# Storing the first shared results from ScalarE's queue, and a third pair of staging buffers

## Chip, cores and metric

The kernel runs on one core of a Trainium2 chip. Its time is the device time in microseconds (us) of one execution; several executions are timed and the median is given. The engines are called PE (TensorE, matmuls), DVE (VectorE), ACT (ScalarE), POOL (GpSimd) and SP (SyncE, which here only issues DMAs); SPq and ACTq are the instruction queues of SP and ACT.

## What is computed

The reference is one block of a network over an input of 4 batches of 1024 tokens with 256 features, all float32. It has two halves.

```
x = x + layernorm(mixer(layernorm(x)))           # linear, conv, scan over tokens, gated linear
x = x + layernorm(ffn(layernorm(x)))
def ffn(x):                                      # 4096 tokens of 256 features
    xn = layernorm(x) * gamma + beta
    top 2 of 8 experts per token, weights comb
    out = sum over e of comb[:, e] * swiglu(xn, gate_up[e], down[e])     # experts, 1024 hidden
    out = out + swiglu(xn, shared_gate_up, shared_down)                  # shared expert, 256 hidden
```

`swiglu` is `(silu(clip(gate)) * up) @ down`. The change touches the last line: the results of the shared expert and the way in which they reach the sum.

## The kernel before

**Two stages.** The first stage, the mixer (0 to about 478 us of the profile), works through the batches b = 0 to 3; each is two half batches of 512 tokens, numbered k = 2b + half, 0 to 7. Mixer, routing, splitting of the expert weights into a high and a low part, and the shared expert are interwoven here. The second stage (from 478 us) runs the routed experts in slots of 256 or 128 rows and adds their rows into `acc_dram` (named `acc_scratch` in the profile) by indirect DMAs from POOL. The shared expert's results must be in `acc_dram` before these additions begin: they are stored there, not added.

**The order is written out by hand.** `ORDER` is a table with one string for each engine; each word, such as `e0/1`, names a stage, its step and a batch or half batch, and `run` calls them in that order. An engine's queue is served in order, so a word that waits holds back all words behind it. For the change these words matter:

- `g`, `y` on PE: gate and up product (`sh_gate`) and down product (`sh_down`) of the shared expert, for half batch k and half f = 0, 1. `clip`, `times` on DVE and `s` on ACT lie between them.
- `ef/k` on ACT, so `e0/1` for half 0 of half batch 1: `sh_copy`, which copies the down product of 256 tokens from PSUM bank 4 to a staging buffer (128 x 512 float32) and counts `s_out` up. PE's next `y` waits for `s_out`, because it overwrites bank 4.
- `sh/k` on SP: `store_shared`, which for both f waits for `s_out` and stores the buffer (256 KB) to `acc_dram`, counting up `s_stored[buffer][f]` when it has landed.
- `n`, `st`, `xr`, `x` on SP: load the next raw piece of expert weights and store the two split parts of an earlier one; store the mixer's result `x1`; load the residual; load the next batch. `w` on ACT and DVE splits a piece.
- `be`, `exp`, `ln`, `abar`, `hi` on ACT, `dt`, `da`, `ac`, `bx`, `h` on DVE, and `dl`, `A`, `b` on PE: the eight units of the scan over tokens of each batch.

**The staging buffers are borrowed.** `sh` holds two pairs. Pair 0 is `a_cum` and `bx`, which the scan of the next batch writes too; pair 1 is the first half of `x_in`, free once the last batch has been normalised and turned. Half batches 0, 1 and 2 are done inside batches 1, 2 and 3 and use pair 0. So the first scan step of batch b (`acum_unit` and `bx_unit` with n = 0) waits on DVE until the store of half batch b - 1 has landed. Half batches 3 to 7 come at the end and alternate: 3, 5 and 7 use pair 1, 4 and 6 use pair 0. `sh_copy` waits for the last store out of its buffer to land, by `used(k)`.

**Signals before the first use.** The weights `w2`, `w3` and the router each have a semaphore in `w_full_loaded`; PE waits for each at its first use.

Of the kernel before, what the change touches and what calls it, by code (L numbers as in the profile page):

```python
# [12 lines left out]
P = 128  # L13
B, L, D, H = 4, 1024, 256, 512
# [3 lines left out]
HALF = 512  # L18
# [47 lines left out]
def mixer(nc, x, w_e, w_s, weights, full, consts, shared, xs_dram, x1_dram, acc_dram, fill, vec, ident,  # L66
# [3 lines left out]
    with ExitStack() as ctx:  # L70
# [80 lines left out]
        vec_loaded = sem("vec_loaded")  # L151
        w_full_loaded = [sem(f"w_full_loaded{i}") for i in range(len(full))]
        w_hi_ready, w_lo_ready = sem("w_hi_ready"), sem("w_lo_ready")
# [9 lines left out]
        s_clipped, s_silu, s_hid, s_out = sem("sh_clipped"), sem("sh_silu"), sem("sh_hid"), sem("sh_out")  # L163
        s_stored = [[sem(f"sh_stored{i}{f}") for f in range(2)] for i in range(2)]
        stats_seen = sp_seen = pool_seen = sem("mixer_waits_seen")
# [28 lines left out]
        def free(engine, what):  # L194
            if what == "x_ps":
                engine.wait_ge(yn_ready, 2 * B + 1)
            elif what == "gu_ps":
                engine.wait_ge(s_hid, 4 * B)
            elif what == "down_ps":
                engine.wait_ge(s_out, 4 * B)  # L200
                engine.wait_ge(slots_ready, B + 2)
            elif what == "xg":
                engine.wait_ge(s_done, 4 * B + 2)
                engine.wait_ge(cv_ready, 4 * B + 2)
            elif what == "gate":
                engine.wait_ge(xs_lo_ready, 4 * B)
                engine.wait_ge(plan_ready, 1)
            elif what == "tables":
                engine.wait_ge(plan_ready, 2)
            elif what == "x1":  # L210
                engine.wait_ge(x1_stored, 16 + 32 * B)
            elif what == "acc":
                engine.wait_ge(ends_cleared, 16 * (E + 2))
                for i in range(2):
                    for f in range(2):
                        engine.wait_ge(s_stored[i][f], 16 * sum(buf_of(k) == i for k in range(2 * B)))
# [33 lines left out]
        sh = [[a_cum[:, :].rearrange("p (t d) -> p t d", d=D), bx[:, :].rearrange("p (t d) -> p t d", d=D)],  # L250
              [x_in[:, 0:2, :], x_in[:, 2:4, :]]]

# [5 lines left out]
        def round_of(b, half):  # L258

            return (b, 0, LT) if b < B - 1 else (b + half, half * HT, HT)  # L260

        def hid_of(k):
            return hid[0 if k < B - 1 else k % 2]

        def buf_of(k):
            return 0 if k < B - 1 else k % 2

        def sh_of(k):
            return sh[buf_of(k)]

        def used(k):
# [89 lines left out]
        def _(sp):  # L361
# [24 lines left out]
            def store_shared(k):  # L386
                for f in range(2):
                    rows = slice(k * HALF + f * 2 * P, k * HALF + (f + 1) * 2 * P)
                    sp.wait_ge(s_out, 2 * k + f + 1)
                    sp.dma_start(acc_dram[rows, :].rearrange("(t p) d -> p t d", p=P), sh_of(k)[f]).then_inc(s_stored[buf_of(k)][f], 16)  # L390

# [29 lines left out]
            for n in range(1, len(full)):  # L421
                load_weights(w_full, *full[n], w_full_loaded[n])
            for at, src, chunks in shared:
# [44 lines left out]
        def _(pe):  # L468
# [69 lines left out]
            def d_stage(b, half, d):  # L538
# [20 lines left out]
                if d in (2, 3):  # L559
                    o = d - 2  # L560
                    if o == 0:
                        pe.wait_ge(s_ready, 2 * k + 2)
                        if k == 0:
                            pe.wait_ge(w_full_loaded[1], 16)
                    for c in range(DC):
                        i = full(banks[6 + o][:, :], W(w_full, W2_AT, c, D, o * P), s[:, c, :], c == 0, c == DC - 1)
                    i.then_inc(g_done, 1)
                if d in (4, 5):
                    if d == 4:
                        pe.wait_ge(z_ready, k + 1)  # L570
                        if k == 0:
                            pe.wait_ge(w_full_loaded[2], 16)
                    for t in ((0, 1), (2, 3))[d - 4]:
# [21 lines left out]
                if d == 9:  # L595
                    r, first, n = round_of(b, half)
                    pe.wait_ge(xnt_ready, 2 * k + 2)
                    if r == 0:
                        pe.wait_ge(w_full_loaded[3], 16)
                    for t in range(n):  # L600
# [44 lines left out]
        def _(act):  # L645
# [146 lines left out]
            def sh_copy(k, f):  # L792
                act.wait_ge(sd_done, 2 * k + f + 1)
                if used(k):
                    act.wait_ge(s_stored[buf_of(k)][f], used(k))
                nc.scalar.activation(sh_of(k)[f], banks[4][:, :].rearrange("p (t d) -> p t d", d=D), ACT.Copy).then_inc(s_out, 1)

            run("scalar", {"p": split_high, "N": normalise_x, "t": copy_xt, "u": copy_u, "c": conv_middle, "S": silu_cv, "r": round_xs,
# [5 lines left out]
        def _(dve):  # L804
# [221 lines left out]
            def sh_clip(k, f):  # L1026
                dve.wait_ge(sg_done, 2 * k + f + 1)
                if buf_of(k) == 0:
                    dve.wait_ge(h_lo_ready, min(k + 1, B) * NU + 2)
# [752 lines left out]
```

## Time and profile before

| | us |
|---|---|
| median of 3 timed executions | 1136.74 (1132.38 to 1138.24) |
| the profiled execution | 1142.15 |
| span in its profile, first to last instruction | 1140.4 |

The rows quoted further down come from the profiled execution alone. A row of the timeline has the start, the busy time, engine and line, the operation with its output and input, and in brackets the idle time of the engine ahead of it with what ended it.
### The profile page before, as it was taken

The numbers are of one execution on the slowest core, as the hardware profiler recorded it, in microseconds if no ns is written. First come the engines' busy times: TensorE is split into PE (matmuls) and PEld (weight loads), VectorE is DVE, ScalarE is ACT, GpSimd is POOL, SyncE is SP. The second block draws the span as 40 slices with busy tenths as digits, with TensorE's granted clock in tenths as the row PEclk, the third lists the DMA queues.
The fourth block names the chain that finished last, engine by engine and source line by source line (L and its number), as shares of the span: only waits on it lengthen the run. The fifth ranks groups of instructions, "written<-read, shape, count | busy, mean of one in ns | idle before, by whom it ended". The sixth has DMA issues, their size and how long they took to land.

```text
span 1140.4 us, 22452 instructions
## 1 busy us (share of the span) xinstructions
PE 1041.2 (91%) x7042; PEld 917.3 (80%) x7042; DVE 800.2 (70%) x2056; ACT 623.9 (55%) x1269; POOL 286.5 (25%) x302
## 2 busy tenths in 40 slices
PE   3889999989988999799999999999999999999940
PEld 2666677668567666599999999999999999999940
DVE  4987898897968766576666666666666666666645
ACT  6867868776767346254444444454444444444415
POOL 1133123552353163311112121211211211112125
PEclk9899999999988999999999999999999999999975
DMA  8655666875574578957363721736275911368139
GB/s 292 215 203 203 224 210 221 266 264 186 180 250 157 189 258 287 335 174 252 81 251 63 245 37 28 254 76 204 41 235 161 345 32 25 68 207 259 34 94 220
DMA packets 123563, 208.96 MB, mean 183 GB/s; under 512 B 9840, under 2 KB 75120, under 8 KB 123504
## 3 DMA queue, kind: packets, MB, share of 16 engines
q1 hardware_dynamic: 108096, 188.33, 48.1%
q0 software_dynamic: 15408, 19.93, 10.0%
q8 instruction: 27, 0.44, 0.2%
q14 instruction: 32, 0.26, 0.1%
HBM read 357.61 MB, written 85.50 MB: 389 GB/s over the span
## 4 chain that ended last, share of the span: by engine, by line
PE 72%; DVE 8%; issue 5%; SPq 5%; DMA 4%; POOL 3%; ACT 2%; ACTq 0%; DVEq 0%; POOLq 0%
PE bank L479 12%; PE bank L1443 8%; PE bank L1444 8%; PE bank L1445 8%; PE bank L1488 4%; PE bank L1490 4%; PE bank L1489 4%; PE bank L473 4%; PE bank L474 4%; PE bank L475 4%; POOL xs_scratch L1209 2%; DMA w_both<-w_split 2%; SPq L1310 2%; PE bank L1461 1%; PE bank L1459 1%
## 5 line engine op out<-in xcount | busy, mean ns | idle before, releaser
L1392 POOL DMA_INDIRECT acc_scratch<-cv,ids x71 | 111.4, 1569 | 518.0 <-DVE cv L1588 494.2
L1625 DVE TENSOR_SCALAR cv<-bank 128x256 f32<-128x256 f32 x284 | 120.5, 424 | 165.9 <-PE bank L1445 141.0
L1555 ACT ACTIVATE cv<-cv 128x256 f32<-128x256 f32 x284 | 118.4, 417 | 183.8 <-DVE cv L1625 183.2
L1443 PE MATMUL bank<-h_hi,w_both 128*128 128x256 f32 x744 | 208.4, 280 | 4.0 <-DMA w_both<-w_split 2.5
L1444 PE MATMUL bank<-h_hi,w_both 128*128 128x256 f32 x744 | 206.4, 277 | 0.0
L1445 PE MATMUL bank<-h_hi,w_both 128*128 128x256 f32 x744 | 206.2, 277 | 0.0
L1541 ACT ACTIVATE h_lo<-cv 128x256 fp32r<-128x256 f32 x248 | 103.1, 416 | 88.4 <-DVE cv L1628 86.9
L1628 DVE TENSOR_TENSOR cv<-bank,cv 128x256 f32<-128x256 f32 x284 | 120.4, 424 | 41.1 <-ACT cv L1555 35.5
L1443 PEld LDWEIGHTS bank<-h_hi,w_both 128*128 128x128 f32 x744 | 140.1, 188 | 6.9 <-issue 4.7
L1445 PEld LDWEIGHTS bank<-h_hi,w_both 128*128 128x128 f32 x744 | 140.1, 188 | 0.0
L1444 PEld LDWEIGHTS bank<-h_hi,w_both 128*128 128x128 f32 x744 | 139.9, 188 | 0.1
L473 PE MATMUL bank<-xs_hi,w_both 128*128 128x512 f32 x224 | 101.2, 452 | 22.7 <-DVE delta L861 9.6
L1488 PE MATMUL bank<-w_both,h_lo 128*128 128x256 f32 x372 | 103.7, 279 | 0.0
L1606 DVE TENSOR_TENSOR h_lo<-cv,h_lo 128x256 fp32r<-128x256 f32 x248 | 103.0, 416 | 0.5 <-ACT h_lo L1541 0.5
L1490 PE MATMUL bank<-w_both,h_lo 128*128 128x256 f32 x372 | 103.0, 277 | 0.0
L1489 PE MATMUL bank<-w_both,h_lo 128*128 128x256 f32 x372 | 102.9, 277 | 0.0
L474 PE MATMUL bank<-xs_lo,w_both 128*128 128x512 f32 x224 | 91.8, 410 | 0.0
L475 PE MATMUL bank<-xs_hi,w_both 128*128 128x512 f32 x224 | 91.6, 409 | 0.0
L1209 POOL DMA_INDIRECT xs_scratch<-n,slot_now x64 | 69.2, 1081 | 62.2 <-DVE slot_now L999 44.5
L473 PEld LDWEIGHTS bank<-xs_hi,w_both 128*128 128x128 f32 x224 | 44.7, 199 | 41.1 <-DVE delta L861 14.6
L1192 POOL TENSOR_TENSOR h_lo<-h,h_hi 128x512 fp32r<-128x512 f32 x32 | 48.8, 1530 | 112.9 <-ACT h_hi L733 112.8
L1023 DVE TENSOR_TENSOR e_raw<-e_raw,e_high 128x768 f32<-128x768 f32 x64 | 64.7, 1014 | 9.9 <-ACT e_high L785 9.9
(273 smaller groups left out, 2652.1 us busy)
## 6 DMA issues: line engine op xcount, KB each, us to landing
w_both<-w_split SPq DMA_DIRECT2D x180, 512.0 KB
single_ring<-w_split SPq DMA_DIRECT2D x18, 3840.0 KB
w_both<-w_split SPq DMA_DIRECT2D x180, 256.0 KB
single_ring<-w_split SPq DMA_DIRECT2D x18, 1536.0 KB
e_raw<-w_e SPq DMA_DIRECT2D x64, 384.0 KB
w_split<-e_high SPq DMA_DIRECT2D x64, 384.0 KB
w_split<-e_raw SPq DMA_DIRECT2D x64, 384.0 KB
xs_hi<-w_split SPq DMA_DIRECT2D x30, 512.0 KB
```

Of the source, the lines that this page charges most:

```text
L473: nc.tensor.matmul(out, hi, x_hi, start=first, stop=False)
L474: nc.tensor.matmul(out, hi, x_lo, start=False, stop=False)
L475: return nc.tensor.matmul(out, lo, x_hi, start=False, stop=last)
L479: return nc.tensor.matmul(out, w, x, start=first, stop=last)
L1443: nc.tensor.matmul(out, gu_hi[f][:, cols], xg_hi[:, par, c, :], start=c == 0, stop=False)
L1444: nc.tensor.matmul(out, gu_hi[f][:, cols], xg_lo[:, par, c, :], start=False, stop=False)
L1445: k = nc.tensor.matmul(out, gu_lo[f][:, cols], xg_hi[:, par, c, :], start=False, stop=c == DC - 1)
L1488: nc.tensor.matmul(out, hg_hi[:, f % 4, toks], d_hi[f], start=f == 0, stop=False)
L1489: nc.tensor.matmul(out, hg_hi[:, f % 4, toks], d_lo[f], start=False, stop=False)
L1490: k = nc.tensor.matmul(out, hg_lo[:, f % 4, toks], d_hi[f], start=False, stop=f == FC - 1)
L1625: nc.vector.tensor_scalar(half, gate_ps, CLIP, -CLIP, ALU.min, ALU.max).then_inc(clipped, 1)
L1628: nc.vector.tensor_tensor(half, up_ps, half, ALU.mult).then_inc(h_ready, 1)
```

## The change

The copies of half batches 0, 1 and 2 are stored by ACT itself, right behind each copy; the three words `sh/0`, `sh/1` and `sh/2` leave SP's order. ACT first waits for its own copy to be finished. There are three pairs of staging buffers: the second half of `x_in` is pair 2, and half batches 3, 4, 5, 6, 7 use pairs 1, 2, 0, 1, 2. SP still stores half batches 3 to 7, in the same places of its order. The three semaphores of `w2`, `w3` and the router become one that counts all three, and PE's three first uses wait for all three loads. POOL, ahead of the first addition, waits for six store semaphores in place of four. The hidden buffers of the shared expert are chosen as before (`hid_no`).

```
-        w_full_loaded = [sem(f"w_full_loaded{i}") for i in range(len(full))]
+        w_full_loaded = [sem("w1_loaded"), sem("w2_w3_router_loaded")]
-        s_stored = [[sem(f"sh_stored{i}{f}") for f in range(2)] for i in range(2)]
+        s_stored = [[sem(f"sh_stored{i}{f}") for f in range(2)] for i in range(3)]
...
             elif what == "acc":
                 engine.wait_ge(ends_cleared, 16 * (E + 2))
-                for i in range(2):
+                for i in range(3):
...
         sh = [[a_cum[:, :].rearrange("p (t d) -> p t d", d=D), bx[:, :].rearrange("p (t d) -> p t d", d=D)],
-              [x_in[:, 0:2, :], x_in[:, 2:4, :]]]
+              [x_in[:, 0:2, :], x_in[:, 2:4, :]], [x_in[:, 4:6, :], x_in[:, 6:8, :]]]
...
+        def hid_no(k):
+            return 0 if k < B - 1 else k % 2
+
         def hid_of(k):
-            return hid[0 if k < B - 1 else k % 2]
+            return hid[hid_no(k)]
 
         def buf_of(k):
-            return 0 if k < B - 1 else k % 2
+            return 0 if k < B - 1 else (k - 2) % 3
...
+        def shared_rows(k, f):
+            return acc_dram[k * HALF + f * 2 * P:k * HALF + (f + 1) * 2 * P, :].rearrange("(t p) d -> p t d", p=P)
...
             def store_shared(k):
                 for f in range(2):
-                    rows = slice(k * HALF + f * 2 * P, k * HALF + (f + 1) * 2 * P)
                     sp.wait_ge(s_out, 2 * k + f + 1)
-                    sp.dma_start(acc_dram[rows, :].rearrange("(t p) d -> p t d", p=P), sh_of(k)[f]).then_inc(s_stored[buf_of(k)][f], 16)
+                    sp.dma_start(shared_rows(k, f), sh_of(k)[f]).then_inc(s_stored[buf_of(k)][f], 16)
...
                         if k == 0:
-                            pe.wait_ge(w_full_loaded[1], 16)
+                            pe.wait_ge(w_full_loaded[1], 48)
...
                     act.wait_ge(s_stored[buf_of(k)][f], used(k))
                 nc.scalar.activation(sh_of(k)[f], banks[4][:, :].rearrange("p (t d) -> p t d", d=D), ACT.Copy).then_inc(s_out, 1)
+                if k < B - 1:
+                    act.wait_ge(s_out, 2 * k + f + 1)
+                    nc.scalar.dma_start(shared_rows(k, f), sh_of(k)[f]).then_inc(s_stored[buf_of(k)][f], 16)
```

**ACT's queue around the copies of half batch 1** (`e0/1` and `e1/1`, in batch 2). `a_cum<-bank` and `bx<-bank` are the two copies, `decay` is the exponential `abar`, `e_high<-e_raw` is a weight split. Line numbers of the changed kernel are some lines higher for the same code. Before:

```order
L755 ACTIVATE g<-bank,nm,rs 128x256 x3
L796 ACTIVATE a_cum<-bank 128x512 [waits sh_stored00,sh_down_done]
L728 ACTIVATE decay<-decay 128x512 [waits da_ready]
L711 ACTIVATE delta<-bank,knee 128x512 [waits da_ready,dl_done]
L717 ACTIVATE delta<-delta,linear 128x512 [waits below_ready]
L796 ACTIVATE bx<-bank 128x512 [waits sh_stored01,sh_down_done]
L785 ACTIVATE e_high<-e_raw 128x768 [waits e_split_stored1,e_raw_loaded1]
```

And in the changed kernel:

```order
L760 ACTIVATE g<-bank,nm,rs 128x256 x3
L801 ACTIVATE a_cum<-bank 128x512 [waits sh_stored00,sh_down_done]
L804 DMA acc_scratch<-a_cum 128x2x256 [waits sh_out]
L733 ACTIVATE decay<-decay 128x512 [waits da_ready]
L716 ACTIVATE delta<-bank,knee 128x512 [waits da_ready,dl_done]
L722 ACTIVATE delta<-delta,linear 128x512 [waits below_ready]
L801 ACTIVATE bx<-bank 128x512 [waits sh_stored01,sh_down_done]
L804 DMA acc_scratch<-bx 128x2x256 [waits sh_out]
L790 ACTIVATE e_high<-e_raw 128x768 [waits e_split_stored1,e_raw_loaded1]
```

Two DMAs have come in, each behind its copy and with a wait for it; nothing else has moved. The same happens at half batches 0 and 2.

**SP's queue around `sh/2`** (end of batch 2's pieces, before the store of x1 named `st0/2`). Before:

```order
L405 DMA w_split<-e_high 128x768 [waits e_lo_made]
L406 DMA w_split<-e_raw 128x768
L390 DMA acc_scratch<-a_cum 128x2x256 [waits sh_out]
L390 DMA acc_scratch<-bx 128x2x256 [waits sh_out]
L384 DMA x_scratch<-xr 128x4x256 [waits x1_ready]
L393 DMA e_raw<-w_e 128x768 [waits e_split_stored0]
```

And in the changed kernel:

```order
L410 DMA w_split<-e_high 128x768 [waits e_lo_made]
L411 DMA w_split<-e_raw 128x768
L390 DMA x_scratch<-xr 128x4x256 [waits x1_ready]
L398 DMA e_raw<-w_e 128x768 [waits e_split_stored0]
L410 DMA w_split<-e_high 128x768 [waits e_lo_made]
```

The two stores and their waits are gone, and the store of x1 and the next piece have moved up by two.

**ACT's queue at the end of the mixer** (`e1/5` to `e1/7`, the last copies). Before:

```order
L796 ACTIVATE x_in<-bank 128x512 [waits sh_stored11,sh_down_done]
L790 ACT_TABLE_LOAD
L790 ACTIVATE delta<-delta 128x512 [waits sh_clipped] x2
L796 ACTIVATE a_cum<-bank 128x512 [waits sh_stored00,sh_down_done]
L796 ACTIVATE bx<-bank 128x512 [waits sh_stored01,sh_down_done]
L796 ACTIVATE x_in<-bank 128x512 [waits sh_stored10,sh_down_done]
L796 ACTIVATE x_in<-bank 128x512 [waits sh_stored11,sh_down_done]
```

And in the changed kernel:

```order
L801 ACTIVATE bx<-bank 128x512 [waits sh_stored01,sh_down_done]
L795 ACT_TABLE_LOAD
L795 ACTIVATE delta<-delta 128x512 [waits sh_clipped] x2
L801 ACTIVATE x_in<-bank 128x512 [waits sh_stored10,sh_down_done]
L801 ACTIVATE x_in<-bank 128x512 [waits sh_stored11,sh_down_done]
L801 ACTIVATE x_in<-bank 128x512 [waits sh_stored20,sh_down_done]
L801 ACTIVATE x_in<-bank 128x512 [waits sh_stored21,sh_down_done]
```

The copies stand in the same places; each now waits for the store of three half batches earlier, where it waited for the one of two earlier.

## Rows read from the trace of the kernel before

**Rows 1.** The page: PE's busy share, and the chain that ended last by engine.

```profile
PE 1041.2 (91%) x7042; PEld 917.3 (80%) x7042; DVE 800.2 (70%) x2056; ACT 623.9 (55%) x1269; POOL 286.5 (25%) x302
...
PE 72%; DVE 8%; issue 5%; SPq 5%; DMA 4%; POOL 3%; ACT 2%; ACTq 0%; DVEq 0%; POOLq 0%
```

**Rows 2.** Waits of SP's queue: line, releaser, us in total, times, longest.

```profile
SPq L390 <- ACT a_cum L796: 5.9, 2, 3.5
```

**Rows 3.** The stores at line 390: duration min/median/max in ns; last row: who waited.

```profile
L390 SPq DMA_DIRECT2D acc_scratch<-a_cum x5: 377/377/952, 132.6 to 476.9; - x5
...
  DVE a_cum L884: 1.0, 1
```

**Rows 4.** ACT's timeline at the copies of half batch 0.

```profile
133.27 0.69 ACT L711 ACTIVATE delta<-bank,knee 128x512 f32<-128x512 f32 x1 [0.71 <-PE bank L475]
...
135.00 0.60 ACT L796 ACTIVATE bx<-bank 128x512 f32<-128x512 f32 x1 [0.29 <-PE bank L479]
135.50 0.84 ACT L785 ACTIVATE e_high<-e_raw 128x768 fp32r<-128x768 f32 x1
```

**Rows 5.** DVE's timeline in the same stretch.

```profile
136.37 0.96 DVE L1023 TENSOR_TENSOR e_raw<-e_raw,e_high 128x768 f32<-128x768 f32 x1 [0.79 <-ACT e_high L785]
...
139.15 0.75 DVE L898 SCALAR_TENSOR_TENSOR bx<-bank,vec,a_cum 128x512 f32<-128x512 f32 x1 [0.51 <-PE bank L475]
```

**Rows 6.** ACT's timeline at the copies of half batch 1.

```profile
229.36 0.60 ACT L796 ACTIVATE a_cum<-bank 128x512 f32<-128x512 f32 x1
229.83 0.64 ACT L728 ACTIVATE decay<-decay 128x512 f32<-128x512 f32 x1
...
232.11 0.60 ACT L796 ACTIVATE bx<-bank 128x512 f32<-128x512 f32 x1 [0.29 <-PE bank L479]
232.66 0.85 ACT L785 ACTIVATE e_high<-e_raw 128x768 fp32r<-128x768 f32 x1
...
239.53 0.69 ACT L711 ACTIVATE delta<-bank,knee 128x512 f32<-128x512 f32 x1 [3.12 <-PE bank L475]
```

**Rows 7.** DVE's timeline in the same stretch.

```profile
233.76 0.95 DVE L1023 TENSOR_TENSOR e_raw<-e_raw,e_high 128x768 f32<-128x768 f32 x1
235.69 1.22 DVE L884 TENSOR_TENSOR_SCAN a_cum<-decay,zeros 128x512 f32<-128x512 f32 x1 [0.98 <-DMA acc_scratch<-a_cum]
```

**Rows 8.** The chain that ended last, same stretch: start, us, what.

```profile
229.99 5.58 DMA acc_scratch<-a_cum
```

**Rows 9.** Half batch 2: timelines of ACT, DVE, PE and SP.

```profile
328.24 0.69 ACT L711 ACTIVATE delta<-bank,knee 128x512 f32<-128x512 f32 x1 [2.32 <-PE bank L475]
...
332.60 0.69 ACT L711 ACTIVATE delta<-bank,knee 128x512 f32<-128x512 f32 x1 [2.39 <-remote]
...
332.23 0.75 DVE L898 SCALAR_TENSOR_TENSOR bx<-bank,vec,a_cum 128x512 f32<-128x512 f32 x1 [4.67 <-remote]
...
333.04 0.79 PE L473 MATMUL bank<-xs_hi,w_both 128*128 128x512 f32 x1 [3.56 <-issue]
...
325.65 2.45 SPq L393 DMA_DIRECT2D e_raw<-w_e  x1
```

**Rows 10.** The splits at line 785 (no releaser is listed under them).

```profile
L785 ACT ACTIVATE e_high<-e_raw x64: 825/833/905, 19.6 to 448.9; 128x768 fp32r<-128x768 f32 x64
```

**Rows 11.** The last copies: timelines of ACT, PE and SP.

```profile
458.52 0.60 ACT L796 ACTIVATE x_in<-bank 128x512 f32<-128x512 f32 x1 [3.51 <-remote]
...
473.96 0.60 ACT L796 ACTIVATE x_in<-bank 128x512 f32<-128x512 f32 x1 [6.18 <-remote]
...
467.92 1.97 PE L479 MATMUL bank<-w_sh,delta 128*128 128x256 f32 x8 [0.78 <-issue]
474.70 3.45 PE L479 MATMUL bank<-w_sh,delta 128*128 128x256 f32 x8 [4.81 <-issue]
...
453.95 1.17 SPq L390 DMA_DIRECT2D acc_scratch<-x_in  x1
...
459.15 0.36 SPq L390 DMA_DIRECT2D acc_scratch<-x_in  x1
```

**Rows 12.** Landing of the store issued at 459.15 (line 390, 456 to 460 us).

```profile
DMA to landing us min/median/max: 2.1/2.1/2.1
```

**Rows 13.** Stretch 476 to 480 us: engines' busy time, granted clock, DMA share, GB/s.

```profile
476.00:480.00 4.00, 4.00 (x22) 3.56 (x21) 0.14 (x1) 0.60 (x1) 0.00 (x0) 0.70 1.06 397
```

More of the change, by code:

```diff
@@ L421, in _ @@
             for n in range(1, len(full)):
-                load_weights(w_full, *full[n], w_full_loaded[n])
+                load_weights(w_full, *full[n], w_full_loaded[1])
             for at, src, chunks in shared:
@@ L571, in d_stage @@
                         if k == 0:
-                            pe.wait_ge(w_full_loaded[2], 16)
+                            pe.wait_ge(w_full_loaded[1], 48)
                     for t in ((0, 1), (2, 3))[d - 4]:
@@ L598, in d_stage @@
                     if r == 0:
-                        pe.wait_ge(w_full_loaded[3], 16)
+                        pe.wait_ge(w_full_loaded[1], 48)
                     for t in range(n):
@@ L1027, in sh_clip @@
                 dve.wait_ge(sg_done, 2 * k + f + 1)
-                if buf_of(k) == 0:
+                if hid_no(k) == 0:
                     dve.wait_ge(h_lo_ready, min(k + 1, B) * NU + 2)
```

6 rows, old and new, of the table ORDER are left out of this document.

## The prediction

> **What bounds the kernel now.** I read the page first: PE is busy for 91% of the span, and the chain of work that ended last lies on PE for 72% of it, on DVE for 8% and on DMAs for 4% [rows 1]. So only what lets PE start earlier, or makes it start later, changes the time. The change touches three short places inside the mixer and its end. I went on to the waits of SP's queue: the stores that leave it were held there for the `a_cum` copies for 5.9 us in two waits [rows 2]. That is time in which SP could not issue the words behind. The view of the stores themselves shows who waits for them: one DVE scan, once, for 1.0 us [rows 3]. The rest had to come from the timelines around each copy.
>
> **Price of a store issued by ACT.** Before, the next ACT instruction starts 0.47 us after the copy does (229.36 and 229.83) [rows 6], which is before the copy's 0.60 us are over. Now the queue must see the copy end: 229.36 + 0.60 = 229.96. SP, which waits for the same signal, issues at 229.99 [rows 8], so 0.03 us more, and the issue of this very transfer takes 0.38 us on SP [rows 3]. The next instruction then starts at about 230.40 in place of 229.83: 0.57 us for each of the six stores. No row shows ACT issuing a DMA; the bounds are 0.38 us, the median above, and 2.45 us, the longest issue nearby in the same stage, on a queue behind a large store [rows 9]. I take the lower, because the six transfers that move are the ones that the median is made of; four of the five `a_cum` stores can't be over 0.95 us [rows 3].
>
> **Half batch 0.** Behind the first copy ACT is idle for 0.71 us until PE has delivered [rows 4]: 0.57 is hidden, and if that cover were gone the scan units would be late by it. Behind the second (135.00) comes a weight split, which DVE waits for (136.37, after 0.79 us idle) [rows 5]. It would start 0.57 later; DVE has 0.51 us of idle time ahead of `bx` at 139.15, where it waits for PE [rows 5]. What is left is +0.06 us.
>
> **Half batch 1.** This is the one place where a store is waited for. It goes out at 229.99 and takes 5.58 us [rows 8], and the first scan of batch 2 starts at 235.69 after 0.98 us of idle time [rows 7]. A store of the same size, with little ahead of it, lands in 2.1 us [rows 12]. On ACT's queue it is not behind the three weight transfers that SP has just issued. I expect it before 235 us. But DVE is then held by its own order: the split ahead of the scan waits for ACT's `e_high`. ACT is late by 0.57 - 0.29 = 0.28 us at the second copy (0.29 us of idle time ahead of it [rows 6]) and by 0.28 + 0.57 = 0.85 behind it: `e_high` ends at 232.66 + 0.85 + 0.85 = 234.36, DVE's split runs from 234.38 to 235.33, and the scan starts at 235.36. That is 0.33 us earlier than before. Bounds: with ACT's lateness at zero, DVE could go on at 233.76 + 0.95 = 234.71, so -0.98 us; and if the store lands no sooner than now, it is +0.07. ACT's own lateness ends in the 3.12 us of idle time before 239.53 [rows 6].
>
> The Trainium skill, DMA: Bandwidth & Descriptors, section Issuing engines are not separate DMA queues, says that DMAs of all queues share the same 16 engines and interleave, so that a second issuing engine saves only issue time. It also says (Queues, rings and completion order) that each engine takes turns between queues by packets. By the first alone this term would be about 0; by the second the store overtakes the backlog, as I assume. No run here shows ACT's queue yet.
>
> **Half batch 2.** Behind both copies ACT has long idle times, the second of 2.32 us before 328.24 [rows 9], so 0.57 costs nothing. DVE's `bx` at 332.23 has waited for 4.67 us, and this instruction waits for PE's product and for the second store of half batch 2. Here the rows must be read together: ACT's L711 at 332.60 ended a wait in the same moment with the same label "remote", and its code waits for PE and DVE alone, never for a store [rows 9]. PE's signals were late in this stretch, whatever the modelled ends say. So I put this wait down to PE and take 0. Bounds: 0, and -3.56 us, PE's idle time before 333.04, if it was the store [rows 9].
>
> **SP without three waits.** The pieces of weights and the store of x1 are issued up to 5.9 us earlier in all [rows 2]. What they feed never waits: none of the 64 splits on ACT has an idle time with a releaser listed [rows 10]. I take 0; what hides it is the two pieces that are loaded ahead. If it failed, ACT would show waits for `e_raw`. The merged weight semaphore costs 0: those loads are issued in the first 11 us, and the first use is 70 us later. POOL's two extra waits lie ahead of its first addition, hundreds of rows off PE's path: 0.
>
> **The third pair.** Copies of half batches 5 to 7 can wait for a landing. The candidate is `e0/7` at 473.96, idle for 6.18 us before it [rows 11]; it wants the store issued at 453.95. The store issued after it on the same queue, at 459.15 [rows 11], landed within 2.1 us [rows 12], so by 461.3, and the earlier one had 20 us. `e1/5` at 458.52 wants a store of about 440. Both waits were for PE's product, which was late as in half batch 2. Three pairs take away a wait that was not there: 0. The bound on the other side: PE waits 4.81 us for this copy where its usual wait there is 0.78, so 4.0, and then runs at a granted clock of 0.70 in that stretch [rows 13], with 3.45 us for what took 1.97 [rows 11], so 1.5 more: -5.5 us.
>
> **Sum.** +0.06 - 0.33 = -0.3 us. The rows are of an execution of 1142.15 us (span 1140.4), 5.4 us above the median of 1136.74, so the sum is carried over to the median: 1136.4 us. About half a percent, 5.7 us, is what can be told from no change.
>
> **Rivals.**
> *The buffers did hold ACT.* For it speaks that both long waits labelled "remote" in the end stage stand before copies into `x_in` [rows 11], that is pair 1. Against it stand the landing times above, and the same label on an instruction that waits for no store [rows 9]. It would give -0.3 - 5.5: 1130.9 us, just past the mark; with the wait of half batch 2 as well, 1127.4 us. Chance 0.22 for both together.
> *ACT's queue is held at the issue.* One DMA in this stage took 2.45 us to issue [rows 9]; two queues that issue at once could do this to each other. Then ACT loses 0.57 + 2.07 = 2.64 us a store, and the covers of 0.71, 0.51, 0.29 and 0.98 us are too small [rows 4 to 7]: 4 x 2.64 - 2.49 = +8.1 us, and 0.3 from the last store (2.64 - 2.32), so 1145.1 us. It decides from about 1.9 us an issue, as (5.7 + 2.49) / 4 = 2.05 lost, less 0.19 that is not issue. For it: transfers of SP are issued in the same microseconds (229.99 is right behind three). Against: these six took 0.38 us there. Chance 0.16.
> The Trainium skill, Perfetto Trace Analysis, section DMA Instruction — HWDGE, speaks for this rival: the block that generates descriptors is shared by the two queues and locked by one at a time, and the lock wait counts in the issue's duration.
> *The stores stay behind the backlog.* If ACT's queue gives no earlier landing, half batch 1 gives +0.07 and the time is 1136.9 us: it can't be told from the forecast, and is part of it.
>
> **How the numbers follow.** No change that can be told: 0.62; faster 0.22; slower 0.16. The range takes in the forecast's case and reaches to the near edges of both rivals: 1129.5 to 1142.0 us.
>
> **What would show it.** Right: six DMA rows on ACT of about 0.4 us, the scan of batch 2 waiting for DVE's own split rather than for a store, the waits before the last copies still there or gone without any relation to stores, PE's idle time in the mixer the same. Wrong: issues on ACT over 1.9 us; `e0/7` starting right behind PE's product in every execution and the kernel 5 us faster; or ACT waiting for `e_raw`. What I could have missed is a shift of the DMA traffic against PE's late stretches, whose cause the trace does not name.

## The result: 0.42% slower, and the profile after

| | us |
|---|---|
| median before, 18 executions | 1137.12 (1130.56 to 1139.96) |
| median after, 18 executions | 1140.80 (1135.49 to 1146.58) |
| ratio after to before | 1.0042, 95% interval 1.0025 to 1.0060: 2.8 to 6.8 us more |
| profiled execution after | 1135.49, span 1133.7 |

The profiled execution of after is the shortest of its 18, that of before (1142.15) is longer than any of the 18. So the two spans can't be subtracted; the rows are compared stretch by stretch. The forecast was 1136.4 us, no change that can be told.

The page of the changed kernel, chain and queues (q10 is the queue that ACT issues to):

```profile
PE 67%; DVE 8%; DMA 6%; SPq 6%; issue 5%; ACT 4%; POOL 3%; another core or an unknown queue 0%; ACTq 0%; DVEq 0%; POOLq 0%
...
q10 hardware_dynamic: 1632, 1.57, 0.4%
```

PE's share of the chain is down from 72%, DMA's up from 4% to 6% [rows 1]. Two stores of f1 are new on it, 4.86 and 6.50 us; the rest of the difference lies in other DMAs and is not followed here. The view of the six stores that ACT now issues (duration min/median/max in ns, then who waited, us and times):

```profile
L804 ACTq DMA_DIRECT2D acc_scratch<-a_cum x3: 366/366/397, 130.5 to 320.7; - x3
L804 ACTq DMA_DIRECT2D acc_scratch<-bx x3: 366/366/383, 133.5 to 325.4; - x3
...
  DVE bx L906: 5.5, 2
  DVE a_cum L892: 0.6, 1
```

The issue costs what it cost on SP (0.37 us), but three waits of DVE stand behind the stores, where there was one [rows 3]; two of them are for `bx`, the stores of f1. The first, at half batch 0, on ACT, SP, DVE and PE:

```profile
132.90 0.60 ACT L801 ACTIVATE bx<-bank 128x512 f32<-128x512 f32 x1 [0.29 <-PE bank L484]
133.53 0.38 ACTq L804 DMA_DIRECT2D acc_scratch<-bx  x1
134.02 0.85 ACT L790 ACTIVATE e_high<-e_raw 128x768 fp32r<-128x768 f32 x1 [0.52 <-ACT bx L801]
...
131.99 0.34 SPq L398 DMA_DIRECT2D e_raw<-w_e  x1
132.37 0.43 SPq L410 DMA_DIRECT2D w_split<-e_high  x1
132.85 0.43 SPq L411 DMA_DIRECT2D w_split<-e_raw  x1
133.39 0.59 SPq L371 DMA_DIRECT2D x_in<-x  x1
...
138.51 0.75 DVE L906 SCALAR_TENSOR_TENSOR bx<-bank,vec,a_cum 128x512 f32<-128x512 f32 x1 [1.33 <-DMA acc_scratch<-bx]
145.14 0.75 DVE L906 SCALAR_TENSOR_TENSOR bx<-bank,vec,a_cum 128x512 f32<-128x512 f32 x1 [1.88 <-PE bank L480]
...
139.97 0.50 PE L478 MATMUL bank<-xs_hi,w_both 128*128 128x512 f32 x1 [3.01 <-DVE delta L869]
```

The same place in the kernel before:

```profile
135.62 0.38 SPq L390 DMA_DIRECT2D acc_scratch<-bx  x1
136.05 0.47 SPq L393 DMA_DIRECT2D e_raw<-w_e  x1
...
140.62 0.50 PE L473 MATMUL bank<-xs_hi,w_both 128*128 128x512 f32 x1 [1.56 <-DVE delta L861]
...
144.21 0.75 DVE L898 SCALAR_TENSOR_TENSOR bx<-bank,vec,a_cum 128x512 f32<-128x512 f32 x1 [0.30 <-PE bank L475]
```

SP, which no longer waits for the copies, has issued the three transfers of a weight piece (each 384 KB) and a load of `x` before ACT issues its store. In the kernel before, SP held all four back until the store was out, and `bx` at 139.15 did not wait for it [rows 5], so it had landed within 3.53 us. Now the store of 256 KB lands 4.86 us after its issue, DVE's `bx` waits 1.33 us for it, and PE, which needs DVE's next product, is idle for 3.01 us. The packets of the two queues in 134 to 136 us and in 136 to 138 us (packets, MB, share of the 16 engines):

```profile
q1 hardware_dynamic: 272, 0.74, 97.2%
...
q1 hardware_dynamic: 312, 0.48, 63.9%
q10 hardware_dynamic: 271, 0.26, 38.9%
```

In the first two microseconds not one packet of ACT's queue was moved; its first ones were between 136.5 and 137 us, 3 us after the issue. Then came a second price. The stretches of 2 us from 138 us (length, then busy time of PE, PEld, DVE, ACT and POOL, granted clock, DMA share, GB/s):

```profile
138.00:140.00 2.00, 0.03 (x1) 0.03 (x1) 1.49 (x3) 2.00 (x5) 0.00 (x0) 1.00 0.96 281
140.00:142.00 2.00, 2.00 (x9) 1.59 (x10) 1.97 (x4) 0.27 (x2) 0.00 (x0) 0.84 1.03 415
142.00:144.00 2.00, 2.00 (x7) 1.71 (x7) 1.23 (x2) 1.97 (x4) 0.00 (x0) 0.50 0.22 60
144.00:146.00 2.00, 2.00 (x8) 1.59 (x8) 0.86 (x2) 1.97 (x4) 0.00 (x0) 0.81 0.61 187
```

After its idle time PE ran at the lower of its two clocks (0.50, 1.2 GHz) for a while, and the second `bx` waited 1.88 us for PE. A short measure for this place is the time from ACT's copy of f1 to DVE's second `bx`: 132.90 to 145.14, 12.24 us. In the kernel before it is from 135.00 (the copy ahead of the 135.50 of [rows 4]) to 144.21, 9.21 us. So 3.03 us are lost here. By the added idle time alone PE would be 3.01 - 1.56 = 1.45 us late; the rest, 1.6 us, goes with the lower clock. In a later profile of the same kernel (c_after_timed) the clock did not fall, and there the place lost 1.67 us with 3.24 - 1.56 = 1.68 us of added idle time.

At half batches 1 and 2 the chain shows:

```profile
230.57 5.70 DMA acc_scratch<-a_cum
...
325.40 6.50 DMA acc_scratch<-bx
```

The first is no quicker than the 5.58 us of SP's queue [rows 8]. Behind the second, DVE's `bx` of batch 3 waits 4.12 us; before, it had waited 4.67 us for something "remote" at the same place [rows 9].

### The profile page after: what moved, and what is told of

Its sections match the earlier page's. It is cut to its first block, busy times and chain, and to the rows that moved or that the text cites. A ratio compares the mean times of both kernels' runs of the same rounds, so it can differ in the third digit from the quotient of the medians.

```text
span 1133.7 us, 22451 instructions
## 1 busy us (share of the span) xinstructions
PE 1037.2 (91%) x7042; PEld 914.1 (81%) x7042; DVE 801.4 (71%) x2056; ACT 624.7 (55%) x1269; POOL 286.7 (25%) x302
## 4 chain that ended last, share of the span: by engine, by line
PE 67%; DVE 8%; DMA 6%; SPq 6%; issue 5%; ACT 4%; POOL 3%; another core or an unknown queue 0%; ACTq 0%; DVEq 0%; POOLq 0%
PE bank L1451 9%; PE bank L1453 8%; PE bank L1452 8%; PE bank L484 8%; PE bank L1496 4%; PE bank L1498 4%; PE bank L1497 4%; PE bank L478 4%; PE bank L480 3%; PE bank L479 3%; POOL xs_scratch L1217 2%; PE bank L1469 1%; PE bank L1467 1%; PE bank L1468 1%; PE bank L1438 1%
```

## Experiments

Each ratio is to the kernel before on the same chip, beside it. There were five groups, each measured side by side on one chip of its own: (1) e1 to e4, (2) e5, e6, e8 and c_before, (3) e9, e10, e11 and c_after, (4) e12, e13, e14 and c_after_timed, (5) e15 and e16. "Traffic theory" is: the store is late because SP, freed of its waits, sends other transfers first. Its rivals: ACT's queue is slow by itself, ACT's own delay is the cost, or the third pair is.

### One part at a time

**e1_act_two_pairs**: ACT's stores without the third pair.

```
-            return 0 if k < B - 1 else (k - 2) % 3
+            return 0 if k < B - 1 else k % 2
```

> The ACT-queue stores alone, with two pairs of buffers as before. Traffic theory (without its waits SP sends four transfers ahead of the store of half batch 0 f1; the store lands later, DVE's first bx of batch 1 waits, PE idles 3.0 us in place of 1.6 and its clock falls): the stores carry the whole loss, +3 to +6 us on before (ratio 1.003 to 1.005), bx near 138.5 waits over 1 us for the store. Queue theory (a store by ACT is slower by itself): the same. Pair theory (the third pair or its order of transfers costs it): within 1 us of before.

Measured: 1.0044 (1.0016 to 1.0072). The stores carry the loss. In its profile the `bx` waited longer still, for 2.61 us, behind a store that took 6.12 us:

```profile
139.97 0.75 DVE L906 SCALAR_TENSOR_TENSOR bx<-bank,vec,a_cum 128x512 f32<-128x512 f32 x1 [2.61 <-DMA acc_scratch<-bx]
...
141.43 0.79 PE L478 MATMUL bank<-xs_hi,w_both 128*128 128x512 f32 x1 [4.28 <-DVE delta L869]
```

**e2_sp_three_pairs**: the third pair alone.

```
+ sh/0, sh/1, sh/2 in SP's order again
-                if k < B - 1:
-                    act.wait_ge(s_out, 2 * k + f + 1)
-                    nc.scalar.dma_start(shared_rows(k, f), ...)
```

> Three pairs alone; SP stores half batches 0 to 2 from its old places. Traffic and queue theories: within 1.5 us of before (ratio 0.999 to 1.001), no wait of DVE for a bx store in batches 1 and 3. Pair theory: +3 to +6 us. If the buffers did hold ACT at the end of the mixer: 3 to 5 us faster.

Measured: 0.9996 (0.9975 to 1.0018). The pair theory falls, and so does the rival that the buffers held ACT (its 3 to 5 us would be a ratio of 0.9974 or less).

**e3_act_hold**: ACT stores, and SP waits where it used to, sending nothing.

```
+ sh/0, sh/1, sh/2 in SP's order again
                     sp.wait_ge(s_out, 2 * k + f + 1)
+                    if k < B - 1:
+                        continue
                     sp.dma_start(shared_rows(k, f), ...)
```

> The changed kernel, but SP still waits for each of the six copies at its old places (it sends nothing there). Traffic theory: the stores land in about 3 us again, DVE's first bx of batch 1 waits for PE or for the 0.6 us that ACT is late, PE's clock stays at 1.0 there: 0 to +1.5 us on before. Queue theory: landing still 4.8 us or more and +3 to +6 us. If both count: +2 us, landing between.

Measured: 0.9999 (0.9981 to 1.0017). The store still took 4.11 us, not the 3 us that I had expected, but the wait of `bx` was 0.58 us, and PE kept its clock. SP sent the piece 0.03 us behind ACT's store (133.28 and 133.25); with both on SP's queue it went 0.43 us behind, and the store landed within 3.53 us. So some 0.6 us or more stay even without anything ahead. Whether that is the smaller distance or the second queue, no run separates:

```profile
138.94 0.50 PE L480 MATMUL bank<-xs_hi,w_both 128*128 128x512 f32 x1 [2.27 <-DVE delta L871]
...
140.00:142.00 2.00, 2.00 (x12) 1.69 (x11) 1.97 (x4) 1.05 (x2) 0.00 (x0) 1.00 0.89 179
```

**e4_sp_k0**: half batch 0 back to SP.

```
+ sh/0 in SP's order again
-                if k < B - 1:
+                if 0 < k < B - 1:
```

> The changed kernel, but half batch 0 is stored by SP at its old place; 1 and 2 by ACT. Both theories on place: the 3.0 us at 137 to 145 us come back, +1 to +2.5 us on before remain. If half batches 1 and 2 cost most: +3.5 us or more. If they cost nothing: within 1 us of before.

Measured: 0.9998 (0.9981 to 1.0016), so -2.2 to +1.8 us, where I had expected 1 to 2.5 us to remain. On this chip no loss is seen once half batch 0 is back on SP.

### Is it ACT's queue, or what goes first?

**e5_sp_behind**: the kernel before, without any store by ACT; only SP's order is changed.

```
- n1/1 sh/0 n2/1 x0/2
+ n1/1 sh0/0 n2/1 x0/2 sh1/0      (sh0: f = 0 alone, sh1: f = 1 alone)
```

> The kernel before (no store on ACT's queue, two pairs, ACT not late) with one edit: SP sends the three transfers of a piece and the load of x ahead of the store of half batch 0 f1, as the changed kernel does in time. Traffic theory: DVE's first bx of batch 1 waits 1 to 3 us for this store, PE idles over 3 us there and its clock falls: +3 to +5 us. Queue theory (only a store sent by ACT is slow) and lateness theory (ACT's 0.63 us is what counts): within 1 us of before, PE idle there 1.56 us.

Measured: 1.0056 (1.0029 to 1.0083).

```profile
133.68 5.66 DMA acc_scratch<-bx
...
139.46 0.75 DVE L898 SCALAR_TENSOR_TENSOR bx<-bank,vec,a_cum 128x512 f32<-128x512 f32 x1 [2.76 <-DMA acc_scratch<-bx]
...
140.92 0.80 PE L473 MATMUL bank<-xs_hi,w_both 128*128 128x512 f32 x1 [3.81 <-DVE delta L861]
```

A loss as large as that of the change, without ACT's queue: the queue theory is not needed for it. The order is harder than in the changed kernel, though. Here the load of `x` goes out 1.01 us ahead of the store (132.67 and 133.68), there 0.14 us; e10_sp_behind_piece below leaves it behind.

**e6_x_later**: the changed kernel, the load of `x` later.

```
- n2/1 x0/2 n3/1 n4/1 x1/2
+ n2/1 n3/1 n4/1 x0/2 x1/2
```

> The changed kernel with the 512 KB load of x of batch 2 moved behind the next two pieces, so that 1.15 MB in place of 1.65 MB stand against the store of half batch 0 f1. Traffic theory: the store lands 0.7 to 1.5 us earlier than the 4.86 us of the changed kernel, PE idles 2.3 us or less, no fall of its clock: 2 to 4 us faster than the changed kernel, 0 to +2 us on before. Queue theory: as the changed kernel, +3 to +6 us.

Measured: 0.9997 (0.9967 to 1.0026), but the profile does not show why. The store took 4.74 us, not 3.4 to 4.2, PE was idle for 2.90 us and its clock fell; copy to second `bx` is 12.12 us, 2.9 more than before. What the load of `x` does seems to hang on its distance. The kernels with this order that issue it 0.14 us ahead of the store (the profile first shown: 133.39 and 133.53; c_after_timed) have a landing of 4.86 and 5.08 us; those that issue it 0.29 and 0.33 us ahead (e1_act_two_pairs, c_after) have 6.12 and 6.17 us. Held against the first two, leaving it out gains little; against the others, 1.4 us. The chip's executions of before were scattered (1132.5 to 1149.7), so the time itself is inconclusive: the interval, -3.8 to +3.0 us, holds the 2.9 us.

**e10_sp_behind_piece**: as e5_sp_behind, but the load of `x` stays behind the store.

```
+ n1/1 sh0/0 n2/1 sh1/0 x0/2
```

> The kernel before with only the three transfers of one piece (1.13 MB) ahead of the store of half batch 0 f1, the 512 KB load of x stays behind it. If the landing goes by the bytes ahead: 0.5 MB less at 0.38 to 0.42 MB/us is 1.2 to 1.4 us earlier than with all four, so bx waits 1.3 to 1.6 us in place of 2.76, PE idles 2.4 to 2.7 us, and it is +1 to +3 us on before. If any transfer ahead costs the same: +4 to +6 us as with all four.

Measured: 1.0010 (0.9989 to 1.0031). In one queue the bytes ahead do count: 4.33 us in place of 5.66, a wait of 1.43 us in place of 2.76, PE idle 2.49 us, all as expected. The clock fell here too; copy to second `bx` is 11.72 us (134.05 to 145.77), so 2.5 us of loss in this profile, and an interval (-1.2 to +3.5 us) that holds it and no loss as well. This is the order on one queue that is nearest to the changed kernel's.

**e12_late_only**: is ACT's delay enough?

```
+                step = CW // 3 if (b, n) == (1, 3) else CW
+                for at in range(0, CW, step):     # three pieces of 256 columns
+                    i = nc.scalar.activation(e_high[..., at:at + step], e_raw[..., at:at + step], ACT.Copy)
+                i.then_inc(e_hi_made, 1)          # once, behind the last piece
```

> The kernel before; only the weight split behind the second copy of half batch 0 is done as three ACT instructions of 256 columns, so that it ends 0.5 to 0.6 us later, as behind a store issued by ACT. The stores stay on SP. Prediction's step (DVE has 0.51 us of cover): DVE's bx at 139 us is 0.1 us late at most, PE idles 1.6 to 1.7 us, the clock stays at 1.0, the time is within 0.5 us of before. Lateness theory (it is ACT's delay and not the landing): PE idles 2.1 us or more and it is +2 to +4 us.

Measured: 1.0000 (0.9982 to 1.0018). DVE's split waits 0.98 us in place of 0.79, a delay of 0.2 and not of the 0.5 to 0.6 that I wanted; `bx` takes it out of its cover (0.32 us in place of 0.51), and PE's idle time is unchanged. So the cover is there, tried with a third of ACT's real delay (DVE's split waits 1.42 us behind ACT's stores):

```profile
134.35 0.96 DVE L1026 TENSOR_TENSOR e_raw<-e_raw,e_high 128x768 f32<-128x768 f32 x1 [0.98 <-ACT e_high L787]
136.95 0.75 DVE L901 SCALAR_TENSOR_TENSOR bx<-bank,vec,a_cum 128x512 f32<-128x512 f32 x1 [0.32 <-PE bank L475]
...
138.42 0.50 PE L473 MATMUL bank<-xs_hi,w_both 128*128 128x512 f32 x1 [1.56 <-DVE delta L864]
```

### The same place again, and the clock

**e9_hold_k0** and later **e14_hold_k0_again**: SP waits at half batch 0 alone. **e13_act_hold_again** is e3_act_hold once more; **c_after** and **c_after_timed** are the changed kernel, **c_before** the kernel before.

```
+ sh/0 alone in SP's order, as a wait that sends nothing
```

> The changed kernel, but SP waits for the two copies of half batch 0 at its old place (it sends nothing there); half batches 1 and 2 are left as changed. Traffic theory with all of the loss at this one place: bx of batch 1 waits 0.6 us or less for the store, PE idles 2.3 us in place of 3.0, no fall of its clock at 140 to 146 us, and the time is within 1.5 us of before. If half batches 1 and 2 carry a part: +2 to +4 us.

> The hold at half batch 0 alone again. Execution theory: as the hold at all three, 0 to +2.5 us on before, and at least 1.5 us faster than the changed kernel beside it. Theory that half batches 1 and 2 carry a part: +3 to +5 us on before, as near to the changed kernel as last time.

> The hold at half batches 0 to 2 again. If the clock's fall is a matter of the execution: after 2.1 to 2.4 us of PE idle time at 140 us it falls in some profiles and not in others, and this kernel and the hold at half batch 0 alone agree within their intervals (0 to +2.5 us on before). If half batches 1 and 2 carry a part: this one is 2 us or more faster than the hold at half batch 0 alone, again.

> The changed kernel once more, for a second profile. The wait of bx for the store is there again, 1.0 to 2.7 us, PE idles 2.7 to 4.3 us ahead of it and its clock falls: 3 to 5 us between 134 and 148 us against before.

> The changed kernel as the yardstick on this chip: +3.5 to +6 us on before; the first bx of batch 1 waits 1 to 2.7 us for its store and PE's clock falls.

> The kernel before once more, for a second profile. If its 6.2 us of idle time ahead of the copy of half batch 7 f0 belonged to the two pairs of buffers it stands here too; if it was a chance of one execution it is 2 us or less. At 139 us: PE idle 1.56 us, clock 1.0.

| kernel | ratio (95%) | landing of f1 | wait of `bx` for it | PE idle | copy to second `bx` | clock falls |
|---|---|---|---|---|---|---|
| SP stores half batch 0 at its old place (9 profiles) | | | 0 | 1.56 | 9.19 to 9.21 | no |
| after, profile first shown | 1.0042 (1.0025 to 1.0060) | 4.86 | 1.33 | 3.01 | 12.24 | yes |
| c_after | one execution | 6.17 | 2.67 | 4.33 | 13.52 | yes |
| c_after_timed | 1.0079 (1.0053 to 1.0105) | 5.08 | 1.56 | 3.24 | 10.87 | no |
| e1_act_two_pairs | 1.0044 (1.0016 to 1.0072) | 6.12 | 2.61 | 4.28 | 14.59 | yes |
| e3_act_hold | 0.9999 (0.9981 to 1.0017) | 4.11 | 0.58 | 2.27 | 9.89 | no |
| e13_act_hold_again | 1.0011 (0.9992 to 1.0031) | 4.01 | 0.48 | 2.17 | 9.82 | no |
| e9_hold_k0 | 1.0040 (1.0015 to 1.0065) | 4.00 | 0.47 | 2.16 | 11.38 | yes |
| e14_hold_k0_again | 1.0055 (1.0031 to 1.0079) | 3.92 | 0.38 | 2.07 | 9.71 | no |

All times in us, each from the rows of its own profile. Two things follow. The loss at half batch 0 is 1.7 to 5.4 us with SP freed, and 0.5 to 2.2 us with SP held. And whether the clock falls is not settled by the idle time: it did not in one profile with 3.24 us, but did in one with 2.16 us, and with 2.17 us in another it did not. Here are PE's row and two stretches of e9_hold_k0, to be held against e3_act_hold above:

```profile
140.18 0.50 PE L480 MATMUL bank<-xs_hi,w_both 128*128 128x512 f32 x1 [2.16 <-DVE delta L871]
...
140.00:142.00 2.00, 1.82 (x6) 1.39 (x7) 1.97 (x4) 1.32 (x3) 0.00 (x0) 0.81 0.97 308
142.00:144.00 2.00, 2.00 (x8) 1.76 (x7) 1.44 (x3) 1.81 (x3) 0.00 (x0) 0.50 0.90 298
```

But the hold at half batch 0 alone stayed 0.4 to 0.55% slow twice, where the hold at all three was not. On one chip, side by side, that is 1.0055 against 1.0011. The two intervals just meet (1.0031). So half batches 1 and 2 very likely carry a part on some chips, where e4_sp_k0 had shown none on its chip.

### Half batches 1 and 2, each alone

**e15_act_k2** and **e16_act_k1**: as e1_act_two_pairs, with the other half batches back on SP.

```
-                if k < B - 1:
+                if k == 2:        (e16: k == 1)
```

> Two pairs; only half batch 2 is stored by ACT's queue and taken from SP's order, 0 and 1 stay with SP. Theory that half batch 2 carries a part: the store of its f1 lands 5.4 us or more after its issue in place of 4.5 us or less, the first bx of batch 3 waits 3 us or more for it in place of 2 us, and it is +1.5 to +4 us on before. If it is hidden as the prediction had it: within 1 us. On a chip where that bx waits 4 us in the kernel before too, nothing shows.

> Two pairs; only half batch 1 is stored by ACT's queue. The store of f0 has the same three transfers ahead of it in both kernels, so the first scan of batch 2 waits 0.6 to 1.3 us as before: within 1 us of before, PE's idle time ahead of 238 us 1.6 to 3 us. If the prediction's step (ACT's store overtakes the backlog) held: the store lands in 4 us or less and 0.3 to 1 us come back. If ACT's lateness costs at the second copy: +1 us or more.

Measured: 1.0025 (1.0003 to 1.0046) for half batch 2, 0.9986 (0.9968 to 1.0004) for half batch 1. First half batch 2 stored by ACT, from e15_act_k2, chain, DVE and PE:

```profile
324.71 6.68 DMA acc_scratch<-bx
...
331.88 0.75 DVE L906 SCALAR_TENSOR_TENSOR bx<-bank,vec,a_cum 128x512 f32<-128x512 f32 x1 [4.31 <-DMA acc_scratch<-bx]
...
332.68 0.79 PE L478 MATMUL bank<-xs_hi,w_both 128*128 128x512 f32 x1 [3.20 <-DVE bx L906]
```

And the same place in e16_act_k1, where SP stores it:

```profile
323.24 0.75 DVE L906 SCALAR_TENSOR_TENSOR bx<-bank,vec,a_cum 128x512 f32<-128x512 f32 x1 [1.64 <-DMA acc_scratch<-bx]
...
324.04 0.50 PE L478 MATMUL bank<-xs_hi,w_both 128*128 128x512 f32 x1 [0.53 <-DVE bx L906]
```

It looks like the same loss a second time: SP has sent a piece (321.70 to 323.08 in e15_act_k2) ahead of ACT's store. From the copy of f1 to this `bx`, SP's kernels of groups 3 to 5 take 5.06 to 5.59 us, those in which ACT stores with SP freed 6.18 to 7.80 us. But that it is the order alone is not shown here. In e13_act_hold_again, where ACT stores and SP waits at this place too, it is 6.15 us with a landing of 5.03 us, about as in c_after (6.18 and 5.06 us) and more than the 3.95 to 4.47 us of a store on SP's queue. So a part belongs to a store on ACT's queue with SP's transfers sent 0.05 us behind it. In groups 1 and 2, and in the first profile of before, SP's kernels took 8.11 to 8.23 us there (five profiles), because PE's product came late for a reason that no row names; those in which ACT stores took no longer, 7.40 to 8.10 us (e1, e3, e4, e6, and the profile after first shown). At half batch 1 nothing changes: both kernels send a piece ahead of the store, and 5.51 us in e16_act_k1 answers to the 5.58 us of [rows 8].

### Two tries at a faster order

**e8_sh1_first** (from e2_sp_three_pairs): the store of half batch 1 ahead of the piece. **e11_between**: between the load of the piece and its two stores.

```
- xr1/1 n0/2 sh/1 n1/2
+ xr1/1 sh/1 n0/2 n1/2                                        (e8)
+ load of n0/2, store f0, the two stores of n0/2, store f1     (e11)
```

> Three pairs, SP stores everything, and the store of half batch 1 stands ahead of the piece of weights that it stood behind. If a store lands by what was sent ahead of it, it takes 3 us or less in place of 5.6 to 6.3, the first scan of batch 2 waits for no store, and 1 us comes back: -0.5 to -2 us on before. If the landing doesn't depend on it: as before, and up to +2 us if the piece of weights is now late.

> Three pairs, SP stores everything; the store of half batch 1 f0 goes out behind the load of the next piece but ahead of that piece's two stores. It has 0.38 MB ahead of it in place of 1.15, so it lands 1.5 to 2.5 us sooner than the 5.6 to 6.3 us, the first scan of batch 2 waits for no store, and the piece is not late (no wait of ACT for e_raw): 0.4 to 1.0 us come back at 235 us, -0.3 to -1.5 us on before in all. If the piece's own stores are then late: the next loads wait for them, and it is slower.

Measured: 1.0043 (1.0014 to 1.0072) and 0.9995 (0.9975 to 1.0014). In e8_sh1_first the scan no longer waits for the store, but the piece itself is late: ACT waits for it, DVE for ACT, and PE is idle for 5.64 us behind them:

```profile
237.47 0.84 ACT L790 ACTIVATE e_high<-e_raw 128x768 fp32r<-128x768 f32 x1 [5.09 <-DMA e_raw<-w_e]
```

In e11_between the scan waits for no store and the piece is not late; a wait of 0.27 us for the store of f1 is left. PE's idle time there is 0.95 us, but between 0.49 us (e15_act_k2) and 2.45 us (c_before) in kernels whose order at this place is the old one, so no gain is shown. No version was found that beats the kernel before.

## Why the prediction was wrong

**What held.** The price of a store on ACT: 0.37 to 0.40 us of issue against the 0.38 assumed, and the instruction behind starts 0.62 us later than before (134.02 - 132.90, against 135.50 - 135.00) against 0.57. The rival of a queue held at the issue falls. DVE's cover ahead of `bx` exists (e12_late_only). The third pair changes nothing (e2_sp_three_pairs); the long wait of `e0/7` was no wait for a buffer. With two pairs it stood again in c_before, at 4.61 us, but four profiles with three pairs (after, e2, e3, e4) have 3.90 to 4.04 us of it too, one copy later, and e12_late_only, with two pairs, has none over 2.15 us. The merged semaphore showed nothing.

**The step that failed** is "SP without three waits", taken as 0. It asked only what SP's earlier transfers feed. It did not ask what they delay. It also counted only the waits for the copies into `a_cum` [rows 2]. The one that mattered stands in another row of the same view, the waits for the copies of f1; its longest, 2.6 us, is at half batch 0. In the changed kernel the piece goes out 1.49 us behind the store of f0 (130.50 and 131.99), so it was the wait for f1 that had held it back:

```profile
SPq L390 <- ACT bx L796: 5.0, 2, 2.6
```

This wait had an effect that no view lists: it kept SP's next transfers behind the store. Without it a piece of 1.13 MB goes first. Giving the waits back takes the loss away: 0.9999 and 1.0011 (e3_act_hold, e13_act_hold_again), where the changed kernel beside the second has 1.0079. And sending more ahead of the store on SP's queue alone costs 1.0056 (e5_sp_behind); with the piece alone ahead (e10_sp_behind_piece) the profile shows a loss of 2.5 us and the time, 1.0010, neither a loss nor none. What the hold leaves at half batch 0 in the profiles, 0.5 to 2.2 us, is the second half of the step: nothing was put down for a store that shares the DMA engines with transfers sent right behind it on the other queue.

**Half batch 0, "+0.06 us".** The sum had ACT's delay of 0.57 us against DVE's cover of 0.51 and no landing of the store at all, since nothing waited for it before (it had 3.53 us to land). The landing was 4.9 to 6.2 us, the wait 1.3 to 2.7 us, and the clock made it up to 5.4 us in all.

**Half batch 1, "-0.33 us".** It rested on a store on ACT's queue that is not behind SP's transfers. It is: 5.5 to 7.0 us in the nine profiles in which ACT stored it and the scan waited for it, 5.1 to 6.3 us on SP's queue. e16_act_k1 gives -1.6 us with an interval of -3.6 to +0.5, so neither a gain nor a loss is shown. The Trainium skill, DMA: Bandwidth & Descriptors, section Issuing engines are not separate DMA queues, says that the DMAs of all issuing engines run on the same 16 engines and that a second one saves only the time of issuing. These landings agree, and I had put it aside. The turns between queues of the same page (section Queues, rings and completion order) I had read as overtaking. The trace does not show turns for transfers that were already on their way: 272 packets of SP's queue and none of ACT's in 134 to 136 us.

**Half batch 2, "0, bounds 0 and -3.56 us".** The bounds had no loss in them. PE's late product, which I took as what sets this place, is a matter of the chip or the execution; where it isn't late, storing by ACT here costs 2.8 us (0.3 to 5.2, e15_act_k2).

**The sum.** -0.3 us was forecast, +4.8 us (2.8 to 6.8) measured. That it came out inside the forecast's range (1129.5 to 1142.0 us) is luck: the range was drawn for the two rivals, and both fell. The profiles give 1.7 to 5.4 us at half batch 0, and between 0.6 us less and 1.6 us more up to `bx` at half batch 2. On the chip of c_after_timed the loss of the median was 6.0 to 11.8 us, more than its profile shows at the two places (10.87 - 9.20 = 1.7 us, and 6.82 us against a mean of 5.2, so 1.6 us). But the profiled execution was a short one: 1130.86 us, 3.4 us above the median of before beside it and 4.3 us below its own median of 1135.14. The 3.3 us fit that execution; what the longer ones lost, perhaps at a lower clock, no profile shows. Why PE's products came late at 332 us in groups 1 and 2 stays open too.

## What to carry to other kernels

A wait in the queue that sends transfers is also a gap in the traffic. Before taking it away, list what will be sent in that gap, and which small transfer with a reader close behind it will then be second. A second issuing engine did not get a store past a backlog here; the order of issue did. And a store on the second queue, sent first, still landed 0.4 us or more later than on the old one, with the other queue's transfers right behind it. Where a term says "nothing waits for it", put a number on the slack and ask what it becomes once the neighbours move.

## What the runs showed of the hardware

- With 1.13 MB of SP's queue on its way for about a microsecond, ACT's queue moved none of its packets for 2 us, and then 271 in the next two. The store landed 4.74 us after its issue without a 512 KB load ahead of it, 4.86 and 5.08 us with the load issued 0.14 us ahead, and 6.12 and 6.17 us with it 0.29 and 0.33 us ahead.
- With nothing ahead and the same transfers 0.03 us behind, on the other queue, it landed in 3.92 to 4.11 us (four profiles); on SP's own queue, with them 0.43 us behind, within 3.53 us.
- PE's granted clock fell to 0.50 after 2.16 us of idle time in one profile and stayed at 1.00 after 3.24 us in another of the same place; after 1.56 us it never fell in nine profiles. Where it fell, the place cost 1.5 to 2.8 us more than the added idle time.
- The kernel before had medians of 1136.5 and 1138.2 us on the chips of groups 1 and 2, and of 1125.8 to 1127.4 us on those of groups 3 to 5.
